# A two-layer block kernel with routed experts on one core: weights of the first 22 blocks from DRAM, bias and scale on ScalarE, wider VectorE operations, a new order of all queues

## The reference, cut to what matters

```python
x = L0_attn_x                                   # (8, 256, 256)
mod = (silu(L0_c) @ L0_wmod).reshape(8, 6, 1, 256)
sa, ca, ga, sb, cb, gb = ...                    # six rows for each sequence; |ga|, |gb| at least 0.25
x = x + ga * attn16(layernorm(x) * (1 + ca) + sa)      # 16 heads of 128, causal softmax
x = x + gb * dense_experts(layernorm(x) * (1 + cb) + sb)   # shared expert + 2 of 8 experts
mod = (silu(L1_c) @ L1_wmod).reshape(8, 6, 1, 256)
x = x + ga * linear_attn(layernorm(x) * (1 + ca) + sa)     # elu + 1 features, cumulative
h = layernorm(x) * (1 + cb) + sb
t = h * rsqrt(mean(h * h) + eps) * norm_w              # 2048 tokens
G = softmax over the top 4 of 16 of (t @ gate_w.T + gate_b)
hid = t @ w1[e].T + b1[e]                               # 512 wide, expert e
act = a * sigmoid(1.702 * a) * (b + 1)   # a = min(hid[::2], 7), b = clip(hid[1::2], -7, 7)
x = x + gb * (h + sum over e of G[e] * (act @ w2[e].T + b2[e]))
```

## Time and profile before

| what | us |
|---|---|
| median of 3 runs (1025.41 to 1028.8) | 1026.29 |
| span of the profiled execution | 1024.1 |
| PE busy over the span | 961.4 |
| DVE busy over the span | 724.0 |
| ACT busy over the span | 673.0 |

### The profile page before, as it was taken

The page is one execution under the profiler, slowest core; times in us unless marked ns, Lnnn a source line. Parts: engine busy times, 40 slices in busy tenths (PEclk is TensorE's granted clock), DMA queues, the critical chain, the costliest instruction groups (busy, mean ns, idle before and its releaser), DMA issues.

```text
span 1024.1 us, 20507 instructions
## 1 busy us (share of the span) xinstructions
PE 961.4 (94%) x6020; PEld 817.2 (80%) x6020; DVE 724.0 (71%) x2545; ACT 673.0 (66%) x1944; POOL 427.7 (42%) x450
## 2 busy tenths in 40 slices
PE   7999999999999999999999999997888989999980
PEld 4769878888987887887788788886667879999970
DVE  3565656777777777778678777875888868888870
ACT  2656767668668757867776876793744657777750
POOL 3323421332371363156136315414145665656673
PEclk9999999999999999999999999998999999999995
DMA  9926993895699620021012004226357899999954
GB/s 306 304 93 207 377 377 113 306 377 188 232 368 375 233 85 2 1 74 64 1 54 77 9 2 168 74 114 241 93 157 179 224 253 231 220 226 224 221 119 82
DMA packets 93725, 180.53 MB, mean 176 GB/s; under 512 B 9949, under 2 KB 29085, under 8 KB 92717
## 3 DMA queue, kind: packets, MB, share of 16 engines
q1 hardware_dynamic: 73467, 148.55, 43.7%
q0 software_dynamic: 18800, 30.30, 13.3%
q10 hardware_dynamic: 1346, 0.36, 0.2%
HBM read 77.71 MB, written 107.99 MB: 181 GB/s over the span
## 4 chain that ended last, share of the span: by engine, by line
PE 82%; DVE 7%; issue 3%; DMA 2%; POOL 2%; ACT 1%; ACTq 0%; DVEq 0%; SPq 0%; POOLq 0%
PE bank L1101 12%; PE bank L1065 10%; PE bank L1037 10%; PE bank L1110 5%; PE bank L1055 5%; PE bank L1027 5%; PE bank L1016 4%; PE bank L987 3%; PE bank L893 3%; PE bank L1056 3%; PE bank L902 3%; PE bank L1046 2%; PE bank L1026 2%; PE bank L971 2%; PE bank L1009 2%
## 5 line engine op out<-in xcount | busy, mean ns | idle before, releaser
L1896 POOL TENSOR_TENSOR RB<-RB 128x512 f32<-128x512 f32 x64 | 66.7, 1042 | 276.2 <-DVE RB L1675 276.0
L1101 PE MATMUL bank<-RB 128*128 128x128 f32 x1264 | 154.9, 276 | 4.9 <-ACT RB L1373 2.0
L1101 PEld LDWEIGHTS bank<-RB 128*128 128x128 f32 x1264 | 148.0, 192 | 7.7 <-ACT RB L1373 2.9
L1366 ACT ACTIVATE RB<-RA,nw 128x512 f32 x158 | 105.5, 715 | 44.7 <-PE bank L1101 16.3
L1065 PE MATMUL bank<-RA,RB 128*128 128x256 f32 x512 | 132.5, 381 | 0.0
L1037 PE MATMUL bank<-RA 128*128 128x256 f32 x512 | 121.4, 380 | 0.0
L1037 PEld LDWEIGHTS bank<-RA 128*128 128x128 f32 x512 | 94.9, 191 | 14.8 <-issue 3.2
L1065 PEld LDWEIGHTS bank<-RA,RB 128*128 128x128 f32 x512 | 91.5, 191 | 12.9 <-issue 2.3
L1872 POOL TENSOR_TENSOR qs<-qs,half 128x4 f32<-128x4 f32 x64 | 65.6, 1025 | 63.6 <-DVE qs L1684 55.9
L1110 PE MATMUL bank<-RB,BC 128*128 128x256 f32 x316 | 82.1, 383 | 3.7 <-DVE BC L1802 3.6
L1267 ACT ACTIVATE RB<-bank 128x256 f32<-128x256 f32 x128 | 48.7, 381 | 44.0 <-PE bank L1056 43.3
(11 more groups left out here) (251 smaller groups left out, 2392.4 us busy)
## 6 DMA issues: line engine op xcount, KB each, us to landing
xsD<-BC SPq DMA_DIRECT2D x17, 4232.0 KB, 32.9
RB<-in_w2b SPq DMA_DIRECT2D x79, 256.0 KB, 3.5
RB<-xsD SPq DMA_DIRECT2D x61, 264.5 KB, 3.6
BC<-modD SPq DMA_DIRECT2D x16, 512.0 KB, 4.3
X<-xsD SPq DMA_DIRECT2D x18, 264.5 KB, 3.3
RA<-in_w SPq DMA_DIRECT2D x2, 2048.0 KB, 7.3
RA<-in_w SPq DMA_DIRECT2D x6, 512.0 KB, 8.7
RA<-in_L_attn_Wq SPq DMA_DIRECT2D x1, 2048.0 KB, 13.7
```

Source lines behind the costliest of these rows:

```text
L1101: m = pe.matmul(ps[:, 128 * j:128 * j + 128], WS[:, n % 2, c, 128 * j:128 * j + 128], XT[:, n % 2, c * 128:c * 128 + 128], start=(c == 0), ...
L1366: m = act.activation(WS[:, n % 2, c, :], W1[:, bass.ds(r, 1), c, :].rearrange("p a n -> p (a n)"), ACT.Copy, scale=nw[:, c:c + 1])
L1896: pool.tensor_tensor(sq, qrow, qrow, ALU.mult).then_inc(mine("q_sq", p), 1)
```

## The change

1. **First weights of blocks 0 to 21** no longer come through `w_in`. A new stage `wx` (SP) moves the block's expert from DRAM, by its number, straight into `WS[n % 2]`, 512 KB a block; it waits for `wo` of head 127 and for `h_mm` of block n - 2. `norm_w` is applied in `x_out` instead, now two ACT operations.
2. **`w12`'s last step** is cut into seven pieces of one expert each, which stand behind `wx` of blocks 2 to 8 in the plan; they are needed from block 22 on, where `w_in` stays.
3. **Bias on ScalarE**: in blocks 0 to 21 ACT adds it in two new stages, `e_h` and `e_u` (two operations of 128x128 each, PSUM to SBUF), and `e_a` and `e_b` on DVE become one `min` of 128x256 each, SBUF to SBUF.
4. **Norm and modulation** of layer 1 (all sequences) and of sequence 7 in layer 0: `(x - mean) * (1 + c)` in one operation and `* rs + s` in the next, on DVE; the mean part doesn't wait for POOL's `ln_rs`. Before it was three steps. `res` is two operations over both halves of a sequence, where there were four. `den` saves one small operation.
5. **Order**: allowances have two values each, before and behind `wo` of head 127, some durations of the table are others, and so all five queues are in a new order. PE keeps its 1265 stages. SP has 234 stages instead of 206.

```diff
+ALLOWED = {"keys": (0.04, 3.968), "query": (0, 0.167), "first": (0.1, 0.148), "shared": (0.04, -0.269), ...}
...
+ALLOWED = {"keys": (0.04, 3.968), "query": (0, 0.167), "first": (0.1, 0.148), "shared": (0.04, -0.269), "dense": (0, 0.052), "linear": (0.08, 0.129), "late": (0.1, -1.959), "route": (0.1, 0.186), "gain": (0.1, -0.085), "count": (0.1, 0.385), "weights": (0.1, -0.854), "token": (0.2, 0.302), "unit": (0.1, -3.143), "block": (0.2, 0.2), "turn": (0.18, -0.08)}
...
         yield do("ln_var", k, b, after=after)
         yield do("ln_rs", k, b)
+
+    def scaled(k, b, before, then):
+        yield do("ln_var", k, b)
...
+        yield do("h_mm", n, bank=2 + n % 2, first=True, after=[("wx", n)] + [("h_mm", n - 1)] * (n > 0))
+        yield do("e_h", n, bank=2 + n % 2, after=[("res", 0, NB - 1), ("s_x", NB - 3, 1)] * (n == 0) + [("e_act", n - 2)] * (n >= 2) + [("e_u", n - 1)] * (n > 0))
+        p.chain("block", upper(n))
+        yield do("e_a", n)
         yield do("e_tanh", n, after=[("e_g", n - 2)] * (n >= 2))
         yield do("e_g", n)
...
+    def upper(n):
+        yield do("e_u", n, bank=2 + n % 2, last=True, after=[("e_h", n)] + [("y_mm", n - 3)] * (n >= 3))
+        yield do("e_b", n)
...
     def weights_in():
-        for n in range(FIRST + 2):
-            yield do("w_in", n, aside=True, after=[("w12", 2), ("n_bi", int(n >= FIRST))] + [("h_mm", n - 2)] * (n >= 2))
+        for n in range(FIRST, FIRST + 2):
+            yield do("w_in", n, aside=True, after=[("w12", 1 + len(LATER)), ("n_bi", 1), ("h_mm", n - 2)])
 
...
         for n in range(FIRST):
+            yield do("wx", n, slot=n % 2, by=16, aside=True, after=[("n_bi", 0), ("wo", NU - 1)] + [("h_mm", n - 2)] * (n >= 2))
...
+            def wx(n):
+
+                on.wait_ge(*done("n_bi", 0))
+                on.wait_ge(*done("wo", NU - 1))
+                if n >= 2:
+                    on.wait_ge(*done("h_mm", n - 2))
+                r = sp.value_load(table(0, n), min_val=0, max_val=15)
+                sp.dma_start(WS[:, n % 2, :, :].rearrange("p (a c) n -> p a (c n)", a=1), I["w1"].rearrange("p (e n) -> p e n", e=16)[:, bass.ds(r, 1), :]).then_inc(mine("wx", n), 16)
+
...
+                    e = (6, 7, 8, 9, 11, 13, 15)[i - 2]
+                    parts = ((e, e + 1),)
                 for lo, hi in parts:
                     sp.dma_start(W1[:, lo:hi, :, :].rearrange("p e c n -> p (e c n)"), I["w1"][:, 1024 * lo:1024 * hi]).then_inc(mine("w12", i), 16)
...
-                on.wait_ge(*done("n_bi", n >= FIRST))
-                on.wait_ge(*done("w12", 2))
+                on.wait_ge(*done("n_bi", 1))
+                for i in range(2 + len(LATER)):
+                    on.wait_ge(*done("w12", i))
                 on.wait_ge(L["small1"], 128)
-                if n >= 2:
-                    on.wait_ge(*done("h_mm", n - 2))
+                on.wait_ge(*done("h_mm", n - 2))
                 r = act.value_load(table(0, n), min_val=0, max_val=15)
...
-                act.activation(XT[:, n % 2, :], psum("x_out", n)[:, 0:256], ACT.Copy).then_inc(mine("x_out", n), 1)
+                if n < FIRST:
+                    on.wait_ge(L["small1"], 128)
+                    for c in range(2):
+                        m = act.activation(XT[:, n % 2, 128 * c:128 * c + 128], psum("x_out", n)[:, 128 * c:128 * c + 128], ACT.Copy, scale=nw[:, c:c + 1])
+                else:
+                    m = act.activation(XT[:, n % 2, :], psum("x_out", n)[:, 0:256], ACT.Copy)
+                m.then_inc(mine("x_out", n), 1)
...
+            def e_h(n):
+                if n not in ex:
+                    ex[n] = expert(n)
...
+                for j in range(2):
+                    m = act.activation(AA[:, n % 2, 128 * j:128 * j + 128], psum("e_h", n)[:, 128 * j:128 * j + 128], ACT.Identity, bias=b1[:, j, bass.ds(ex[n], 1)])
+                m.then_inc(mine("e_h", n), 1)
+
+            def e_u(n):
+                if n >= 3:
+                    on.wait_ge(*done("y_mm", n - 3))
+                for j in range(2):
+                    m = act.activation(AB[:, n % 3, 128 * j:128 * j + 128], psum("e_u", n)[:, 256 + 128 * j:384 + 128 * j], ACT.Identity, bias=b1[:, 2 + j, bass.ds(ex[n], 1)])
+                m.then_inc(mine("e_u", n), 1)
...
                 for t in range(2):
-                    m = dve.tensor_scalar(dst[:, t, :], X[:, j + t, :], mv[:, j + t, 0:1], rs[:, j + t, 1:2], ALU.subtract, ALU.mult)
+                    if whole:
+                        m = dve.scalar_tensor_tensor(dst[:, t, :], X[:, j + t, :], mv[:, j + t, 0:1], BC[:, (b % 3, 4 + b % 2)[k // 2], 512:768], ALU.subtract, ALU.mult)
+                    else:
+                        m = dve.tensor_scalar(dst[:, t, :], X[:, j + t, :], mv[:, j + t, 0:1], rs[:, j + t, 1:2], ALU.subtract, ALU.mult)
                 m.then_inc(mine("ln_x", k, b), 1)
...
-
             def f_add(l, b):
-                if not (l == 0 and b < NB - 1):
-                    shift(dve, on, l, b)
+                if l == 0 and b < NB - 1:
+                    return
+                v, j = route(l), 2 * b
+                on.wait_ge(*done("ln_rs", 2 * l + 1, b))
+                on.wait_ge(*done("ln_x", 2 * l + 1, b))
+                if b:
+                    on.wait_ge(*(done("f_t", 0, b - 1) if l == 0 else done("f_x", b - 1)))
...
                     on.wait_ge(*done("h_t", 1, b))
-                for t in range(2):
-                    j = 2 * b + t
-                    dve.tensor_tensor(tmp[:, t, :], ps[:, t * 256:t * 256 + 256], g, ALU.mult).then_inc(ch.sem, ch.up())
-                    on.wait_ge(ch.sem, ch.n)
-                    m = dve.tensor_tensor(X[:, j, :], X[:, j, :], tmp[:, t, :], ALU.add)
-                    if t == 0:
-                        m.then_inc(ch.sem, ch.up())
-                m.then_inc(mine("res", l, b), 1)
+                x = X[:, 2 * b:2 * b + 2, :]
+                dve.tensor_tensor(tmp, pair(ps[:, :]), row(l, b, 0), ALU.mult).then_inc(ch.sem, ch.up())
+                on.wait_ge(ch.sem, ch.n)
+                dve.tensor_tensor(x, x, tmp, ALU.add).then_inc(mine("res", l, b), 1)
...
+                if n < FIRST:
+                    on.wait_ge(*done("e_h", n))
+                    dve.tensor_scalar(AA[:, n % 2, :], AA[:, n % 2, :], 7.0, None, ALU.min).then_inc(mine("e_a", n), 1)
+                    return
                 on.wait_ge(*done("h_mm", n))
-                if n >= 2:
...
-                if n >= 3:
+                if n < FIRST:
+                    on.wait_ge(*done("e_u", n))
+                    m = dve.tensor_scalar(AB[:, n % 3, :], AB[:, n % 3, :], 8.0, None, ALU.min)
+                else:
                     on.wait_ge(*done("y_mm", n - 3))
-                for j in range(2):
+                for j in range(2 * (n >= FIRST)):
                     m = dve.tensor_scalar(AB[:, n % 3, 128 * j:128 * j + 128], psum("e_b", n)[:, 256 + 128 * j:384 + 128 * j], b1[:, 2 + j, bass.ds(ex[n], 1)], 8.0, ALU.add, ALU.min)
```

184 lines of the change are left out of this document (92 added, 92 removed), and 10 rows, old and new, of the table ENGINE.

## The result

The changed kernel takes 1032.51 us (median of 9 runs, 1029.3 to 1035.09) against 1028.11 of the kernel before beside it (9 runs, 1025.41 to 1030.34): a ratio of 1.0039, interval 1.0027 to 1.0051. It is slower by 0.4%, where 1021.8 was forecast, and lies just outside the range of 1016 to 1031. The forecast had counted from 1026.29 us of three runs; the kernel before stands at 1028.11 over nine, so that 1.8 of the 10.7 us between forecast and measurement are a drift of the base. Its profiled execution took 1030.99 us, the span 1028.7.

What follows compares the result with a forecast made beforehand. PE bounds the kernel, and only the fill between the last `wo` and `h_mm` of block 22 loses time, 26 us. Terms -6.3 - 1.0 + 2.8 = -4.5 us, from 1026.3 to 1021.8 us, range 1016 to 1031.

Steps and rivals of the forecast that it cites:

- What bounds it: PE is the bound; only the fill, from last `wo` to `h_mm` of block 22, loses time, 26 us.
- First stretch, -6.3: From the last `wo` to 741 us: earlier first block and full clock, 7.4 us lost in place of 13.7.
- the end of the attention: Ahead of the last `wo`: three moved stages no longer fill PE's gaps, 1.5 us, between 0 and 3.
- The small waits behind: Behind the last `wo`, up to 741 us: many small PE waits, 1.6 us in all.
- Second stretch, -1.0: Middle of the fill, 741 to 779.8 us: less VectorE work and shorter chain, PE's idle 5.5 becomes 4.5 us.
- Third stretch, +2.8: From 779.8 to 828.8 us: waits for `wx` in two buffers, 9.6 us replacing 6.8.
- L: Time for a `wx` load of 512 KB to land, taken as 5.4 us, bounds 4.3 and 8.3.
- the pair of blocks short of 1.6 us: Last part of the fill: two blocks need 8.6 us against 7.0 of PE work; six pairs make 9.6 us.
- the plan has them a block or more ahead: Last part of the fill: `w2x` and `xb` queue behind a waiting `wx` on SP, but early enough; no cost added.
- the third rival: Slower: two `WS` buffers with slow `wx` loads, around 1030 from 6.5 us landing, 1042 at 8.3; chance 0.22.
- ring rival: Two `WS` buffers with slower `wx` loads: gain gone at 6.0 us, 1026 (chance 0.20), or slower from 6.5 (0.22).
- the fourth: In the fill, VectorE operations hold up POOL's eight `f_send`, block 22 2.4 us later: 1024.2, chance 0.08.

Runs made afterwards that it cites:

- three_moved: Kernel before in its own order, with `h_t`, `qk_mm` and `vv_mm` of sequence 6 and their helper stages moved behind the last `wo`: 1028.62 us, 1.0001.
- bias_on_dve: Changed kernel in its own order, with the bias of blocks 0 to 21 back on VectorE as `e_a` and `e_b`: 1032.21 us, 1.0047.
- ring_of_three: Changed kernel, order kept, with `wx` of blocks 0 to 14 taking turns over three buffers instead of two: 1031.51 us, 1.0048.

## Why the prediction was wrong

**What bounds it: right.** PE's lost time in the fill is what the change moves, the loop keeps its 163 us, and the clock of the first stretch is 1.00 instead of 0.86.

**First stretch, -6.3: right in sum.** 35.2 - 30.75 = 4.5 us idle. To that comes what the attention didn't get ahead by, 3.3 - 0.4 = 2.9 us. Together 7.4, the forecast's 7.4 in place of 13.7. Inside it the end of the attention was put at 1.5 and took 2.9: the holes are 0.5 (`three_moved`), one wait of 1.65 us for the PSUM bank of `n_bi` came with the new order. The small waits behind took less than I had given them.

**Second stretch, -1.0: wrong, +1.6.** 7.1 us are lost and not 4.5. The step that failed is that a relieved VectorE shortens PE's waits here. `e_a` and `e_b` took 14.6 us instead of 26.6, so 12 us and not 17 were taken off, though a single `min` has about the 0.3 us that I gave it (0.29 median; one took 1.55). They bought nothing that the times show (`bias_on_dve`). In their place `x_t` waits 3.3 us for `xb` in this stretch and `h_mm` 1.7 for `wx`.

**Third stretch, +2.8: the sign right, the size short, measured +6.0.** 11.2 us were lost where I had 9.6, and another 1.6 by the clock (0.03 x 52.2), which I had at none. L was right (5.3). But the pair of blocks short of 1.6 us, 2.0 + 1.2 + L against 7.0, should have put all 9.6 on `h_mm`, and only 3.7 us name `wx`; 5.4 name `xb`. The sentence that failed is "the plan has them a block or more ahead", as far as `xb` goes: I priced the new load by its own landing and let the old ones land as before, when the DMA engines went from 0.83 to 0.99 busy. `xb` took 1.3 us longer to land from 741 to 780 us, `w2x` 1.0 in the third stretch, and `x_t` waits for `xb` in line.

**The sum.** 7.4 + 7.1 + 11.2 + 1.6 = 27.3 us are lost now against 26 before; the forecast had 21.5. These 5.8 us are 2.6 of the second stretch and 3.2 of the third. The forecast was for the way from the first `q_mm` to `h_mm` of block 22; there the two profiled runs differ by +2.1 us (812.53 against 810.47), where it had -4.5. The rest of the 4.6 us between their spans is the later start of the first `q_mm` (1.1) and the time behind the last `y_mm`, 29.7 us against 28.1; other runs have 26.9 to 30.2 there. Neither hangs on the change as far as I can see, and I can't say whether the medians differ by them too. The profiled execution of the changed kernel also had the highest granted clock of its nine (0.986, the others 0.978 to 0.985), so that its stretches may show less of the clock's price than the median pays.

**Rivals.** By size the outcome is the near end of the third rival, "slower by over 0.3%, around 1030": 4.4 us on 1026.3 are 1030.7. By mechanism it is neither ring rival, since they asked for L of 6.0 or 6.5, and L was 5.3. The third had named what else stood on SP's queue, but priced only the ring. The range ended at 1031 because it was made from L alone. POOL held up by VectorE, the fourth, isn't seen in `f_send`: the eight take 9.2 us from first to last start (9.0 before), and the last starts at 816.0, before at 817.5.

**Open:** what `x_t`'s waits for `xb` cost, and how to be rid of them. In the runs where the kernel before took 1027 to 1028 us they are 6.5 us (`bias_on_dve`) to 12.4 (`ring_of_three`), 8.0 with half the bytes of `wx`, where `xb` lands in 4.3 us over the fill (4.8 in the changed kernel, 3.5 before). Where it took 1038, kernels of that order have 3.6 to 5.3 us, and waits for VectorE stand beside them; so one trace gives them to a few microseconds only. A sixth buffer for the rows, and a third for `wx` with SP's list made for it, were not tried.

## What to carry to other kernels

A load that is added to a stretch whose DMA engines are already 0.8 busy has to be priced for all loads there: here it made small ones late that had been just in time. Another queue for it did not help. Another buffer helps only if the queue's list lets the load go out earlier; look at the issue times before calling it refuted. Fewer bytes in the stretch did help (6.2 and 4.7 us). Where a planner writes the order, an edit that goes through it again measures the planner (9 to 15 us here); keep the list and move single stages to measure the edit. And time taken off an engine counts only where another waits for just that operation: 12 us off VectorE's block stages changed nothing that these runs can tell.
